# Signalling a weight slab's scale two operations into the GpSimd chain, with its other factors under a signal of their own

## The reference

```python
x = x + _L0_xattn_ref(_layernorm(x), ctx, mask, Wq, Wk, Wv, Wo, qn, kn)   # q and k through an rmsnorm, 8 key heads
x = x + _L0_ffn_ref(...)
x = x + _L1_xattn_ref(...); x = x + _L1_ffn_ref(...)
x = x + _L2_xattn_ref(_layernorm(x), ctx, mask, bias, Wq, Wk, Wv, Wo)     # 32 key heads
x = x + _L2_ffn_ref(...)
x = x + _L3_xattn_ref(_layernorm(x), ctx, Wq, Wk, Wv, Wo)                 # 4 key heads
x = x + _L3_ffn_ref(...)
# each attention, per head:
q, k, v = hidden @ Wq, hidden_kv @ Wk, hidden_kv @ Wv
out = softmax(q @ k.T * scale + bias) @ v @ Wo
```

## Time and profile before

| what | value |
|---|---|
| runs | 2570.93, 2571.7, 2572.21 us; median 2571.7 |
| profiled execution | 2575.95 us, its span 2574.0 us |
| TensorE busy | 2318.8 us (90%) |
| VectorE busy | 1352.7 us (53%) |
| ScalarE busy | 1166.2 us (45%) |
| GpSimd busy | 528.5 us (21%) |
| granted clock of TensorE, mean | 0.949 |
| layer 0 / layer 2 / layer 3 attention | about 44 to 700, 1010 to 1812, 1920 to 2486 us |

### The profile page before, as it was taken

The page is one execution under the profiler, slowest core; times in us unless marked ns, Lnnn a source line. Parts: engine busy times, 40 slices in busy tenths (PEclk is TensorE's granted clock), DMA queues, the critical chain, the costliest instruction groups (busy, mean ns, idle before and its releaser), DMA issues.

```text
span 2574.0 us, 40154 instructions
## 1 busy us (share of the span) xinstructions
PE 2318.8 (90%) x14118; PEld 1307.9 (51%) x14118; DVE 1352.7 (53%) x2618; ACT 1166.2 (45%) x2974; POOL 528.5 (21%) x873
## 2 busy tenths in 40 slices
PE   4899899999885977999999999999769899999979
PEld 2565555555442423455555555555534455555545
DVE  5566666666633034555555555555442355555551
ACT  4556555665410222554445544443222465555530
POOL 2332332323120001221212212111200121221130
PEclk8999999999967988999999999999879999999988
DMA  3110110100002021211111111100120001000000
GB/s 111 42 42 22 42 38 27 42 22 18 22 1 98 1 76 48 78 45 60 45 60 55 51 61 44 62 11 11 63 81 1 34 34 48 37 34 34 1 30 33
DMA packets 27622, 106.95 MB, mean 42 GB/s; under 512 B 4353, under 2 KB 12929, under 8 KB 17426
## 3 DMA queue, kind: packets, MB, share of 16 engines
q1 hardware_dynamic: 26962, 104.10, 11.5%
q10 hardware_dynamic: 448, 0.03, 0.0%
HBM read 102.03 MB, written 2.10 MB: 40 GB/s over the span
## 4 chain that ended last, share of the span: by engine, by line
PE 62%; DVE 13%; ACT 12%; issue 10%; POOL 2%; DMA 1%; ACTq 0%; POOLq 0%; SPq 0%; DVEq 0%
PE bank L84 15%; PE bank L86 15%; PE bank L85 15%; ACT m_E L411 2%; PE bank L1232 2%; DVE m_Sm L794 2%; PE bank L1561 2%; PE bank L588 2%; DVE m_x L840 1%; DVE m_nmax L810 1%; ACT m_arena L389 1%; PE bank L1141 1%; ACT m_E L407 1%; ACT m_arena L291 1%; PE bank L1346 1%
## 5 line engine op out<-in xcount | busy, mean ns | idle before, releaser
L734 DVE TENSOR_TENSOR m_arena<-bank,m_arena 128x512 f16<-128x512 f32 x336 | 232.1, 691 | 542.0 <-ACT m_arena L389 541.6
L84 PE MATMUL bank<-m_input_parts,m_arena 128*128 128x512 f16 x1088 | 416.1, 382 | 6.6 <-DVE m_arena L734 2.3
L86 PE MATMUL bank<-m_input_parts,m_arena 128*128 128x512 f16 x1088 | 416.1, 382 | 0.0
L85 PE MATMUL bank<-m_input_parts,m_arena 128*128 128x512 f16 x1088 | 416.1, 382 | 0.0
L411 ACT ACTIVATE m_E<-m_Sm,m_nmax 128x128 f32<-128x128 f32 x512 | 199.1, 390 | 425.4 <-DVE m_nmax L810 249.2
L852 POOL TENSOR_TENSOR m_E<-m_E,m_rinv 128x512 f32<-128x512 f32 x192 | 199.8, 1041 | 908.7 <-DVE m_rinv L825 908.7
L389 ACT ACTIVATE m_arena<-bank 128x512 f16<-128x512 f32 x336 | 199.0, 592 | 249.7 <-PE bank L86 249.2
L84 PE MATMUL bank<-m_wo_t,m_A 128*128 128x512 f16 x768 | 291.1, 379 | 3.1 <-DVE m_x L840 3.1
L85 PE MATMUL bank<-m_wo_t,m_A 128*128 128x512 f16 x768 | 291.1, 379 | 0.0
L86 PE MATMUL bank<-m_wo_t,m_A 128*128 128x512 f16 x768 | 291.1, 379 | 0.0
L84 PE MATMUL bank<-m_arena,m_input_parts 128*128 128x128 f16 (+1 forms) x768 | 197.5, 283 | 1.4 <-DVE m_arena L734 0.9
(11 more groups left out here) (265 smaller groups left out, 4444.7 us busy)
## 6 DMA issues: line engine op xcount, KB each, us to landing
m_raw<-a_q SPq DMA_DIRECT2D x24, 1024.0 KB, 4.9
m_raw<-a_o SPq DMA_DIRECT2D x24, 1024.0 KB, 4.8
m_raw<-a_k SPq DMA_DIRECT2D x9, 1024.0 KB, 4.9
m_raw<-a_v SPq DMA_DIRECT2D x9, 1024.0 KB, 4.9
m_bias_in<-bias SPq DMA_DIRECT2D x64, 128.0 KB, 2.0
m_arena<-f_w SPq DMA_DIRECT2D x4, 1024.0 KB, 5.0
m_arena<-ctx_t SPq DMA_DIRECT2D x2, 2048.0 KB, 7.7
m_x<-x SPq DMA_DIRECT2D x2, 1024.0 KB, 7.0
```

The lines of the kernel that those rows point to most:

```text
L84: pe.matmul(out, lhs[0], rhs[0], start=first, stop=False)
L85: pe.matmul(out, lhs[0], rhs[1], start=False, stop=False)
L86: return pe.matmul(out, lhs[1], rhs[0], start=False, stop=last)
L734: ins = dve.tensor_tensor(self.dest(name, part, 1), self.shaped(bank[m % 2][:, :]), self.dest(name, part, 0), ALU.subtract)
```

## The change

`scales` is put in another order. The product that signals `w_scale` now stands second, straight behind total^-0.5. The total^0.5 follows without waiting for it; then GpSimd waits for its own `w_scale` signal and goes on with the rest. The last operation of each kind signals a new semaphore, `w_fac`. In layer 0 the kinds q and k lose one operation, since they use the finished scale instead of multiplying it anew. `low` on VectorE waits for `w_fac` besides `w_hi`. The counts of the chain per period (`CHAIN`) follow. Nothing else moves; no DMA is added or taken away.

```diff
-    CHAIN = {"dve": {0: 0, 2: 16, 3: 8}, "pool": {0: 23, 2: 17, 3: 12}}
+    CHAIN = {"dve": {0: 0, 2: 16, 3: 8}, "pool": {0: 17, 2: 13, 3: 10}}
...
     def low(self, dve, kind, j, par, count):
         dve.wait_ge(*self.s["w_hi"].by(count))
+        dve.wait_ge(*self.s["w_fac"].by(count))
...
+        fac = s["w_fac"]
         tt(sc, tot, k.c_mhalf, ALU.pow, t)
+        tt(sc, sc, k.c_cw, ALU.mult, t, s["w_scale"])
         tt(inv, tot, k.c_half, ALU.pow, t)
-        tt(inv, inv, k.c_icw, ALU.mult, t)
-        last = lambda: tt(sc, sc, k.c_cw, ALU.mult, t, s["w_scale"])
-        if self.layer == 0 and kind in "qk":
-            tt(k.tmp, sc, k.c_cw, ALU.mult, t)
+        pool.wait_ge(*s["w_scale"].by(slab))
+        if kind == "o":
+            tt(inv, inv, k.c_icw, ALU.mult, t)
...
+            tt(k.osc[:, kp], k.tmp, k.joint[:, 1:2] if self.layer == 3 else k.inv_c[:, 0:1], ALU.mult, t, fac)
+        elif self.layer == 0 and kind in "qk":
+            tt(inv, inv, k.c_icw, ALU.mult, t)
             if kind == "k":
-                tt(k.tmp, k.tmp, k.s_c[:, 0:1], ALU.mult, t)
-            tt(k.tmp, k.tmp, k.tmp, ALU.mult, t)
-            tt((k.eps_q if kind == "q" else k.eps_k)[:, kp], k.tmp, k.c_eps, ALU.mult, t)
...
+                tt(k.tmp, sc, k.s_c[:, 0:1], ALU.mult, t)
+                tt(k.tmp, k.tmp, k.tmp, ALU.mult, t)
+            else:
+                tt(k.tmp, sc, sc, ALU.mult, t)
+            tt((k.eps_q if kind == "q" else k.eps_k)[:, kp], k.tmp, k.c_eps, ALU.mult, t, fac)
...
+        elif self.layer == 3 and kind == "q":
+            tt(inv, inv, k.c_icw, ALU.mult, t)
             tt(k.tmp, inv, k.inv[1][:, 0:1], ALU.mult, t)
             tt(k.tmp, k.tmp, k.joint[:, 1:2], ALU.mult, t)
             tt(k.tmp, k.tmp, k.joint[:, 1:2], ALU.mult, t)
-            tt(k.qk[:, kp], k.tmp, k.c_scale, ALU.mult, t)
...
+            tt(k.qk[:, kp], k.tmp, k.c_scale, ALU.mult, t, fac)
+        else:
+            tt(inv, inv, k.c_icw, ALU.mult, t, fac)
```

More of the change, by code:

```diff
@@ L111, in __init__ @@
         self.NP, self.NK = len(self.pre), len(self.kinds)
-        names = ["raw0", "raw1", "w_ss", "w_tot", "w_scale", "w_hi", "w_lo", "misc", "misc_read",
+        names = ["raw0", "raw1", "w_ss", "w_tot", "w_scale", "w_fac", "w_hi", "w_lo", "misc", "misc_read",
                  "proj", "proj_hi", "proj_lo", "scores", "biased", "top", "exped", "rinv", "probs",
@@ L120, in __init__ @@
         slabs = self.NP + 7 * self.NK + 1
-        totals = dict.fromkeys(("w_ss", "w_tot", "w_scale", "w_hi", "w_lo"), slabs)
+        totals = dict.fromkeys(("w_ss", "w_tot", "w_scale", "w_fac", "w_hi", "w_lo"), slabs)
         totals |= {"raw0": 16 * ((slabs + 1) // 2), "raw1": 16 * (slabs // 2)}
@@ L852, in tt, with scales @@
             pool.tensor_tensor(out, a, b, op).then_inc(sem.sem, 1)
-    def scales(self, pool, kind, j, par, count, t=0):
+    def scales(self, pool, kind, j, par, count, slab, t=0):
         k, s = self.k, self.s
@@ L866, in scales @@
         inv = k.inv["qkvo".index(kind)][:, kp]
+        fac = s["w_fac"]
         tt(sc, tot, k.c_mhalf, ALU.pow, t)
+        tt(sc, sc, k.c_cw, ALU.mult, t, s["w_scale"])
         tt(inv, tot, k.c_half, ALU.pow, t)
-        tt(inv, inv, k.c_icw, ALU.mult, t)
-        last = lambda: tt(sc, sc, k.c_cw, ALU.mult, t, s["w_scale"])
-        if self.layer == 0 and kind in "qk":
-            tt(k.tmp, sc, k.c_cw, ALU.mult, t)
-            if kind == "k":
-                tt(k.tmp, k.tmp, k.s_c[:, 0:1], ALU.mult, t)
-            tt(k.tmp, k.tmp, k.tmp, ALU.mult, t)
-            tt((k.eps_q if kind == "q" else k.eps_k)[:, kp], k.tmp, k.c_eps, ALU.mult, t)
-        if self.layer == 2 and kind == "k":
+        pool.wait_ge(*s["w_scale"].by(slab))
+        if kind == "o":
+            tt(inv, inv, k.c_icw, ALU.mult, t)
+            tt(k.tmp, inv, k.inv[2][:, 0:1] if self.layer == 3 else k.inv[2][:, kp], ALU.mult, t)
+            tt(k.osc[:, kp], k.tmp, k.joint[:, 1:2] if self.layer == 3 else k.inv_c[:, 0:1], ALU.mult, t, fac)
+        elif self.layer == 0 and kind in "qk":
+            tt(inv, inv, k.c_icw, ALU.mult, t)
+            if kind == "k":
+                tt(k.tmp, sc, k.s_c[:, 0:1], ALU.mult, t)
[3 more added lines that the diff above has]
+            tt((k.eps_q if kind == "q" else k.eps_k)[:, kp], k.tmp, k.c_eps, ALU.mult, t, fac)
+        elif self.layer == 2 and kind == "k":
+            tt(inv, inv, k.c_icw, ALU.mult, t)
             tt(k.tmp, inv, k.inv[0][:, kp], ALU.mult, t)
             tt(k.tmp, k.tmp, k.inv_c[:, 0:1], ALU.mult, t)
-            tt(k.qk[:, kp], k.tmp, k.c_scale, ALU.mult, t)
-        if self.layer == 3 and kind == "q":
+            tt(k.qk[:, kp], k.tmp, k.c_scale, ALU.mult, t, fac)
+        elif self.layer == 3 and kind == "q":
+            tt(inv, inv, k.c_icw, ALU.mult, t)
             tt(k.tmp, inv, k.inv[1][:, 0:1], ALU.mult, t)
@@ L910, in pool_ahead @@
             pool.wait_ge(*s["w_lo"].by(j - 1))
-            self.scales(pool, kind, j, 0, j + 1)
+            self.scales(pool, kind, j, 0, j + 1, j + 1)
     def pool(self, pool):
@@ L943, in emit @@
                     pool.wait_ge(*s["w_lo"].by(at(t, self.NK, self.NP + n - 1)))
-                    self.scales(pool, kind, self.NP + n + self.NK * par, pp, at(t, self.misc_per, self.NP + misc + 1), t)
+                    self.scales(pool, kind, self.NP + n + self.NK * par, pp, at(t, self.misc_per, self.NP + misc + 1),
+                                at(t, self.NK, self.NP + n + 1), t)
                 elif e[0] == "k_rms":
```

6 lines of the change are left out of this document (3 added, 3 removed).

## The result

The changed kernel takes 2562.6 us (median of 7 runs, 2561.02 to 2566.31) against 2571.7 us before (7 runs, 2568.88 to 2573.97): 0.31% faster, ratio 0.9969 with a 95% interval of 0.9957 to 0.998. In microseconds of the kernel before that is 8.0, between 5.1 and 11.1; the two medians are 9.1 apart. The forecast was 2564.3.

A forecast was written before the change was run, and what follows sets the result against it. TensorE was taken to set the end in the attention layers, helped only where it stands behind ScalarE's wait for the scale. 5.5 + 1.2 + 0.7 = 7.4 us off gives 2564.3 us, range 2562.2 to 2569.5.

The forecast's parts named there:

- Layer 3: Loop of layer 3, slab q: TensorE's six waits for m_E vanish, 5.5 us.
- The play: Layer 3, slab q: m_E done 0.9 us before TensorE asks, 0.3 us if VectorE's split is delayed 0.6 us.
- The weaker reading: Layer 3: a running m_E might not delay VectorE's split at all, between no delay and 0.6 us.
- VectorE's split grew beyond 2.35 us: Layer 3: sign named in advance that would show the prediction wrong.
- The start of layer 0: Start of layer 0: first projection starts 1.05 to 1.35 us earlier, 1.2 us taken.
- The first period: First period of layer 0: TensorE's wait at L558 shortens by 0 to 0.7 us, 0.7 taken.
- So the 1.9 us of both reach the end: Layer 0: gains of its start and first period, 1.9 us, reach the end, as no timer or transfer holds engines back.
- The sign that was named: End of layer 0: comes 1.9 us earlier if the prediction holds.
- Nothing ahead of layer 2: Ahead of layer 2: no gain, both slabs are made under the feed-forward block and TensorE next waits for the layer norm.
- nothing for the waits: VectorE's 82 added waits: cost taken as 0, upper bound 3.3 us.
- The third rival: Layer 3: VectorE's split holds up running m_E, TensorE waits 0.65 us more six times; 2573.7 us, chance 0.07.
- The lower end of the range: Whole kernel: upper bounds of layer 0's terms and 1 us more, 2562.6 us, rounded to 2562.2.

The follow-up runs named there:

- e1_l3q: Early scale at slab q of layer 3 alone, all else as in the kernel before: 2565.57 us, ratio 0.9968 to the kernel before.
- e4_spot3: Changed kernel, but at slab q of layer 3 the scale comes fourth in its chain instead of second: 2567.68 us, layer-3 stretch 406.64 us, one execution.
- e10_qsum_before: Kernel before, late scale kept, with ScalarE's copy of q's sums in layer 0 moved ahead of a slab's high part: 2563.55 us, ratio 0.9969.
- e3_all_but_l3q: Early scale at every slab except q of layer 3, which stays as in the kernel before: 2570.09 us, ratio 0.999.
- e5_spot5: Changed kernel, but at slab q of layer 3 the scale comes sixth in its chain: 2566.22 us, layer-3 stretch 408.79 us, one execution.
- e2_l0: Early scale in layer 0 alone, all four kinds; layers 2 and 3 as in the kernel before: 2571.79 us, ratio 0.9995.
- e6_mE_late: Changed kernel plus three idle GpSimd products behind slab q's factors in layer 3, so VectorE's split starts before m_E: 2583.61 us, one execution.
- e8_qsum: Changed kernel with ScalarE's copy of q's sums in layer 0 moved ahead of a slab's high part: 2555.29 us, ratio 0.993.
- e9_qsum_first: Changed kernel with ScalarE's copy of q's sums moved still earlier, ahead of its copies of the output block: 2578.37 us, ratio 1.002.

## Why the prediction was right, step by step

**Layer 3**: the mechanism is the one forecast, down to the order of events, and e1_l3q and e4_spot3 show it. The term was sized too small: 5.5 us forecast, 7.4 in the trace. The six idle times of the earlier trace rows are what the records show between the ends of matmuls, and those ends overlap: the last L86 of before starts at 2088.87 and is recorded with 0.38 us, while such matmuls follow each other every 0.22, so TensorE could have gone on at 2089.09 and not at 2089.25. A wait of 0.96 costs 1.12. By that count six waits are 5.5 + 6 x 0.16 = 6.5 us, which is what e4_spot3 gained. The loop's steps fell from 58.05 and 59.21 to 56.86 and 57.83, 1.2 and 1.4 us for each slab. Laid side by side, the two traces show the rest in two places: the transposes behind a wait follow each other 0.06 us closer, and the wait at L84 at the turn of the loop is 0.69 us where it was 0.92. That last one lies between 0.5 and 1.0 us in traces of either kind, so this part may be chance. (What stands ahead of the prediction says that TensorE's busy time counts some time twice. It doesn't; the overlap of the records hides the first 0.16 us of a wait.)

**The play**: "0.9 us, 0.3 if VectorE is held": it is 0.28, and VectorE is held. The weaker reading, that this `m_E` might not hold anything, fell. VectorE's split grew beyond 2.35 us, which the prediction named as a sign that it is wrong. The sign was badly chosen: the prediction's own text allows 0.6 us of delay there, and with 0.28 us of play left TensorE didn't stand for it. How near that was is part luck.

**The start of layer 0**: 1.02 us at the first projection against 1.2, and 1.26 if one counts from the start of GpSimd's chain, which this execution reached 0.24 us later. The split of k and `w_fac` came as forecast in the same way (the chain's end at 42.60, forecast 42.15 to 42.45). The first period was to bring 0.7, and its L558 moved by 0.69 more (1.71 in all). But the first scores came 3.3 us earlier, and that the prediction didn't have. It is the clock: from L84's first start to the first scores pass 31.3 us before and 29.0 after. Behind L558 TensorE of before runs at its lower level, and that of the changed kernel doesn't (windows of before, then of the changed kernel):

```profile
65.30:72.10 6.80, 5.41 (x33) 3.84 (x32) 1.76 (x4) 1.20 (x2) 4.33 (x9) 0.50 0.54 193
68.00:72.00 4.00, 3.34 (x27) 3.28 (x28) 1.76 (x4) 0.61 (x2) 2.00 (x2) 0.50 0.32 121
```

```profile
63.50:66.90 3.40, 2.76 (x7) 0.74 (x5) 1.01 (x3) 1.32 (x2) 2.65 (x8) 0.50 0.81 292
66.90:70.90 4.00, 3.79 (x56) 3.54 (x56) 1.01 (x3) 0.52 (x2) 2.73 (x1) 0.99 0.26 80
```

At first I took the shorter wait (0.69 in place of 1.39) for its cause. But in both traces the clock had fallen ahead of L558, behind a wait of 2.76 and 2.75 us at L551: it is low from 65.3 to 72.1 before and from 63.5 to 66.9 after. The other traces speak against it too: e10_qsum_before, e3_all_but_l3q and e5_spot5 have the wait at 0.69 too and need 31.0 us. With the early scale at the start seven traces of nine are at 28.6 to 29.0 us, with the late one none of three; whether the change favours the short case is open.

**"So the 1.9 us of both reach the end"**: not shown. e2_l0 and e3_all_but_l3q bound what the start brings to between nothing and 4.6 us. The sign that was named, layer 0 ending 1.9 us earlier, doesn't decide it either: it ends 5.0 us earlier in the changed kernel's trace and 0.2 later in those two.

**Nothing ahead of layer 2, nothing for the waits**: right as far as the runs can tell. A met wait costs 0.02 us, and 82 of them 1.4 if they all lay on the path. Ahead of layer 2 no run isolates the change; the stretch that holds it (below) is no shorter with the early scale than with the late one. The third rival, the split that holds up `m_E`, was no straw man. As written, with `m_E` already running, it is refuted: that `m_E` kept its 1.04 us. e6_mE_late shows the same loss with the split first. In layer 3 that cost 15.4 us over the kernel before where I had priced 3.9, since GpSimd stands for the rest of a 2.35 us split and TensorE's clock falls behind it. What kept it away is that `m_E` starts 0.4 us before the split.

**The total**: 8.0 us by the ratio, forecast 7.4. The sum came out close because layer 3 was worth two microseconds more than I wrote and the start perhaps less. The lower end of the range was summed wrongly: 5.5 + 1.35 + 0.7 and 1 us more below 2571.7 is 2563.15, not 2562.6. The measured median lies below that, the 8.0 us by the ratio (2563.7) do not. Of the 14.9 us between the profiled executions 7.4 are layer 3, and no run ties more than a few microseconds of the rest to the change: the stretch from the end of layer 0 to the end of layer 2, in which no wait of TensorE hangs on the change, takes between 1106.7 and 1113.2 us in the twelve traces (1112.6 before, 1109.5 in the changed kernel, 1106.7 in e10_qsum_before, which has the late scale). The layer-3 stretch is 405.4 to 406.0 us in the five traces that have the early scale as the change has it and 412.4 to 413.1 in the four with the late one.

## What to carry to other kernels

Ask of an earlier signal how many of its waits TensorE stands behind (here 6 of 11, in 82), and price such a wait by the spacing of the matmuls, not by the idle time in the records alone. Compare a stretch whose length repeats between traces before believing a difference of whole runs. A wait of TensorE that can't be removed may be worth splitting in two: here that was worth as much as the change, with 1.8 us more idle time in sum. Moving it whole to another place was a loss.

## What the runs showed that I had not expected

- TensorE's granted clock fell behind about half of the waits of 2.05 us in layer 0 (four or five periods of 40.0 to 40.1 us in each of the nine traces with this wait), and behind none of the waits of 1.45 us in e8_qsum and e10_qsum_before. It fell behind 11 of 12 waits of 2.18 us in e9_qsum_first. Which of the equal waits is hit varies from trace to trace. That isn't most of the scatter of the totals: the twelve runs of e10_qsum_before, whose trace has none of these falls inside the loop, spread over 11.4 us, and 23 of the kernel before over 7.2.
- VectorE holds up GpSimd even if GpSimd's operand is one element a partition: such operations took 0.76 to 1.60 us under L1689 instead of 0.19 or 0.55, and 2.3 us inside the 2.35 us split. The other way round it depends on what GpSimd does: `m_E` lengthens the split, the 128x4 product of the earlier trace rows doesn't.
